# State products of a two-layer kernel: B and C spread by DMA instead of TensorE, the B product on GpSimd instead of VectorE, and four heads per maximum and exponential

## The reference, cut to what matters

```python
def step(h, inp):
    dt_t, B_t, C_t, x_t = inp
    dA = jnp.exp(dt_t[..., None] * A)
    h = dA * h + dt_t[..., None] * B_t[:, None, :] * x_t[..., None]
    y = jnp.sum(h * C_t[:, None, :], axis=-1)
    return (h, y)
```

## Time and profile before

| | before |
|---|---|
| median of 3 runs | 1556.84 us (1555.11 to 1557.42) |
| the profiled execution | 1551.08 us |
| its span | 1549.3 us |
| mean granted TensorE clock | 0.894 |
| DMA, mean over the span | 40 GB/s |

### The profile page before, as it was taken

The page is one execution under the profiler, slowest core; times in us unless marked ns, Lnnn a source line. Parts: engine busy times, 40 slices in busy tenths (PEclk is TensorE's granted clock), DMA queues, the critical chain, the costliest instruction groups (busy, mean ns, idle before and its releaser), DMA issues.

```text
span 1549.3 us, 28028 instructions
## 1 busy us (share of the span) xinstructions
PE 1230.7 (79%) x10568; PEld 841.1 (54%) x10568; DVE 1056.9 (68%) x1741; ACT 734.8 (47%) x1420; POOL 273.4 (18%) x277
## 2 busy tenths in 40 slices
PE   4777877689986998789986998689976997679228
PEld 3554444356753576356753576356844675347118
DVE  2343355977688676867688677977698667966864
ACT  1233444555563645455554645555554644453322
POOL 1000010222012110221012110221013110321250
PEclk9799998889997999789987999899988999799659
DMA  5330010011200211011210211012111121002002
GB/s 199 58 41 1 12 43 28 1 26 39 72 32 14 46 49 60 1 25 39 73 32 15 46 54 54 1 25 56 56 32 23 41 69 32 14 9 82 30 0 72
DMA packets 109587, 62.28 MB, mean 40 GB/s; under 512 B 71248, under 2 KB 91504, under 8 KB 109456
## 3 DMA queue, kind: packets, MB, share of 16 engines
q1 hardware_dynamic: 108448, 56.95, 14.2%
q10 hardware_dynamic: 1008, 3.54, 0.6%
HBM read 53.36 MB, written 6.59 MB: 39 GB/s over the span
## 4 chain that ended last, share of the span: by engine, by line
PE 57%; DVE 21%; issue 9%; ACT 9%; DMA 1%; POOL 1%; SPq 0%; ACTq 0%; DVEq 0%; POOLq 0%
PE strips L813 8%; PE strips L798 7%; PE ps L992 7%; PE ps L980 6%; PE attn_out L826 6%; DVE hb L1461 6%; ACT probs L1085 5%; DVE hb L1456 3%; DVE rowmax_B L1314 3%; PE ps L745 3%; PE attn_out L833 2%; DVE rowmax_A L1314 2%; PE ps L754 2%; DVE work L1428 2%; PE ps L763 2%
## 5 line engine op out<-in xcount | busy, mean ns | idle before, releaser
L1085 ACT ACTIVATE probs<-strips 128x1024 f32<-128x1024 f32 x256 | 251.6, 1021 | 133.1 <-PE strips L813 132.7
L1314 DVE TENSOR_REDUCE rowmax_B<-strips 128x4 f32<-128x1024 f32 x192 | 226.0, 1219 | 77.9 <-PE strips L798 77.7
L813 PE MATMUL strips<-qs_b,ks_b 32*128 32x256 f32 x1536 | 130.0, 459 | 33.0 <-ACT probs L1085 30.5
L798 PE MATMUL strips<-ks_b,qs_b 32*128 32x256 f32 x1536 | 124.7, 443 | 37.4 <-ACT probs L1085 25.2
L1461 DVE TENSOR_TENSOR_SCAN hb<-da,hb 128x1024 f32<-128x1024 f32 x64 | 152.3, 2379 | 2.2
L1547 DVE SCALAR_TENSOR_TENSOR work<-hb,ps 128x512 f32<-128x512 f32 x128 | 87.7, 686 | 88.8 <-ACT hb L1215 88.5
L992 PE MATMUL ps<-ze,w_e 128*128 128x256 f32 x512 | 129.6, 388 | 3.3 <-DVE work L1547 1.9
L980 PE MATMUL ps<-w_e,work 128*128 128x128 f32 x1024 | 125.2, 276 | 0.2 <-DVE work L1547 0.2
L980 PEld LDWEIGHTS ps<-w_e,work 128*128 128x128 f32 x1024 | 122.2, 192 | 5.2 <-issue 2.8
L1215 ACT ACTIVATE hb<-ps 128x512 f32<-128x512 f32 x128 | 75.9, 599 | 103.4 <-PE ps L992 101.4
L1174 ACT ACTIVATE da<-gate,a_neg 128x255 f32<-128x255 f32 x256 | 108.3, 499 | 34.1 <-DVE hb L1461 29.0
(11 more groups left out here) (238 smaller groups left out, 1956.6 us busy)
## 6 DMA issues: line engine op xcount, KB each, us to landing
w_e<-in_w_e SPq DMA_DIRECT2D x128, 256.0 KB, 3.1
qs_a<-a_scr SPq DMA_DIRECT2D x8, 512.0 KB, 4.6
ks_a<-a_scr SPq DMA_DIRECT2D x8, 512.0 KB, 4.9
pos<-t_scr SPq DMA_DIRECT2D x8, 264.0 KB, 10.8
a_scr<-qkv_a SPq DMA_DIRECT2D x16, 128.0 KB, 3.7
qs_b<-maxrow_B SPq DMA_DIRECT2D x96, 4.0 KB
x_in<-in_x SPq DMA_DIRECT2D x8, 128.0 KB, 3.1
a_scr<-ks_a SPq DMA_DIRECT2D x2, 512.0 KB, 6.3
```

The costliest lines, as they stand in the source:

```text
L798: mm = pe.matmul(o, strip(qs, b, kind, g, j, qc * P, P), strip(ks, b, kind, g, j, 0, L), start=True, stop=True)
L813: mm = pe.matmul(o, strip(ks, b, kind, g, j, kc * P, P), strip(qs, b, kind, g, j, 0, L), start=True, stop=True)
L1085: act.activation(probs[:, group % 2, 2 * i:2 * i + 2, :, :].rearrange("p h a b -> p (h a b)"), strips[i][:, :], ACT.Exp).then_inc(s_exp, 1)
L1314: dve.tensor_reduce(out=rowmax[kind][:, b % sides_n, k % 2, 2 * i:2 * i + 2, :], in_=strips[i][:, :].rearrange("p (h q t) -> p h q t", h=2 ...
```

## The change: what it does

- B and C are no longer spread by TensorE. ScalarE copies the 32 rows from PSUM to `bc_rows`, a DMA writes them to DRAM (`bc_scr`), and eight DMAs for each sequence read two rows of B and two of C back with a partition step of zero, 512 KB each, into a ring of four (`bc_all`). All are issued by SP. The bf16 split, `sel` and the matmuls of L933 are gone.
- The B product moves from VectorE to GpSimd (stage `input`), two pairs ahead. The C product stays on VectorE and reads C from SBUF.
- Softplus, the tanh of the experts and `h_t` get tiles of their own, and `ze` gets a second half, so waits of layer one on the experts of the sequence before are gone or later.
- `strips` is one tile of 2048 columns; one `top` and one `exp` do four heads.
- The table of numbers is new, with a lane of its own for what comes after `h_t`.

```diff
+BC_RING = 4
-        CELL += [("max", "B", _g), ("top", "B", _g, 0), ("top", "B", _g, 1), ("rows", "B", _g)]
+        CELL += [("max", "B", _g), ("top", "B", _g), ("rows", "B", _g)]
...
-LAYER1 += [("inproj",), ("conv",), ("xc",), ("bcdt",), ("bc",), ("sp_u",), ("sp_z",)]
-LAYER1 += [("state", _k) for _k in range(NS // 2)]
+LAYER1 += [("inproj",), ("conv",), ("xc",), ("bcdt",), ("bc_write",), ("sp_u",)] + [("bc", _k) for _k in range(BC_RING)] + [("sp_z",)]
+LAYER1 += [("input", 0), ("input", 1)]
+for _k in range(NS // 2):
+    LAYER1 += [("state", _k)] + ([("input", _k + 2)] if _k + 2 < NS // 2 else []) + ([("bc", _k + BC_RING)] if _k + BC_RING < NS // 2 else [])
...
 START = {
-    "one": [0, 24262, 48541, 72825, 97082, 121354, 145602, 169496],
+    "one": [0, 24336, 48715, 73062, 97418, 121814, 146122, 171281],
+    "two": [99, 24430, 48842, 73166, 97539, 121895, 146278, 402809],
...
-        strips = [ctx.enter_context(nc.psum_tensor(f"strips{i}", [P, 2 * 512], F32)) for i in range(2)]
+        strips = ctx.enter_context(nc.psum_tensor("strips", [P, 4 * 512], F32))
...
-        sp_abs = work[:, 0, 0:2, :]
-        sp_max = work[:, 0, 2:4, :]
-        sp_u = work[:, 1, 0:2, :]
-        sp_p = work[:, 1, 2:4, :]
+        bc_rows = sb("bc_rows", [2 * NS, L])
+        bc_all = sb("bc_all", [P, BC_RING, 2, 2, L])
+        sp_abs, sp_max, sp_u, sp_p = (sb(n, [P, CH, L]) for n in ("sp_abs", "sp_max", "sp_u", "sp_p"))
...
-        eh_t = hb[:, :, :, :, :].rearrange("p a c j t -> p a (c j) t")[:, :, 0:2, :]
+        eh_t = sb("eh_t", [P, 2, 2, L])
+        bc_scr = nc.dram_tensor("bc_scr", [2 * NS, L], F32).ap()
...
+            def bc_write(b):
+                sp.wait_ge(*bc_done.at(b))
+                past(sp, hc_done, b - 1, NS // 2 - 1)
+                sp.dma_start(bc_scr, bc_rows[:, :]).then_inc(bc_written.of(b), 16)
+
+            def bc_read(b, k):
+                if k == 0:
+                    sp.wait_ge(*bc_written.at(b))
+                if k >= BC_RING:
+                    sp.wait_ge(*hc_done.at(b, k - BC_RING))
+                i = (b * (NS // 2) + k) % BC_RING
+                src = bass.AP(tensor=bc_scr.tensor, offset=2 * k * L, ap=[[0, P], [NS * L, 2], [1, 2 * L]])
+                sp.dma_start(bc_all[:, i, :, :, :].rearrange("p w j t -> p w (j t)"), src).then_inc(bc_in[i], 16)
...
-            def state(b, k):
-                pe.wait_ge(*bc_steps.at(b, 4))
-                for which, base in (("b", 0), ("c", NS)):
-                    o = take(b, (which, k))
-                    for j in range(2):
-                        mm = pe.matmul(...)
-                    mm.then_inc(s_ps, 1)
...
             def bcdt(b):
+                ready(act, b, "bc")
+                past(act, bc_written, b - 1)
+                act.activation(bc_rows[:, :], bank(b, "bc")[0:2 * NS, 0:L], ACT.Copy).then_inc(bc_done.of(b), 1)
                 ready(act, b, "dt")
-                past(act, acc_done, b - 1, EX)
+                past(act, sp_steps, b - 1, 8)
...
             def state(b, k):
-                ready(dve, b, ("b", k))
-                o = bank(b, ("b", k))[:, :].rearrange("p (o j t) -> p o j t", o=1, j=2).to_broadcast([P, CH, 2, L])
-                dve.tensor_tensor(hk, o, dtx[:, :, :].unsqueeze(2).to_broadcast([P, CH, 2, L]), ALU.mult).then_inc(hb_done.of(b), 1)
                 dve.wait_ge(*hb_done.at(b, k))
                 dve.wait_ge(*da_done.at(b, k))
                 dve.tensor_tensor_scan(flat_h, flat_a, flat_h, 0.0, ALU.mult, ALU.add).then_inc(scan_done.of(b), 1)
                 dve.wait_ge(*scan_done.at(b, k))
-                ready(dve, b, ("c", k))
-                dve.tensor_tensor(hk, hk, o, ALU.mult).then_inc(hc_done.of(b), 1)
+                dve.wait_ge(bc_in[n % BC_RING], 16 * (n // BC_RING + 1))
+                c = bc_all[:, n % BC_RING, 1, :, :].unsqueeze(1).to_broadcast([P, CH, 2, L])
+                dve.tensor_tensor(hk, hk, c, ALU.mult).then_inc(hc_done.of(b), 1)
...
+            def state_input(b, k):
+                pool.wait_ge(*dtx_done.at(b))
+                if k >= 2:
+                    pool.wait_ge(*pair_done.at(b, k - 2))
+                n = b * (NS // 2) + k
+                pool.wait_ge(bc_in[n % BC_RING], 16 * (n // BC_RING + 1))
+                c = bc_all[:, n % BC_RING, 0, :, :].unsqueeze(1).to_broadcast([P, CH, 2, L])
+                pool.tensor_tensor(hb[:, k % 2, :, :, :], c, dtx[:, :, :].unsqueeze(2).to_broadcast([P, CH, 2, L]), ALU.mult).then_inc(hb_done.of(b), 1)
```

More of the change, by code:

```diff
@@ L164 @@
+        "two": [],
     },
@@ L422, in hybrid_layers @@
         xc_done = sig("xc_done", 1)
-        bc_steps = sig("bc_steps", 5)
+        bc_done = sig("bc_done", 1)
+        bc_written = sig("bc_written", 1, 16)
+        bc_in = [one(f"bc_in{i}") for i in range(BC_RING)]
         sp_steps = sig("sp_steps", 9)
@@ L777, in take_strips @@
                     user, was, kind, g = STRIP_LIST[at - 1]
-                    for i in range(2):
-                        if was == "max":
-                            pe.wait_ge(*top_done[kind].at(user, 2 * g + i))
-                        else:
-                            pe.wait_ge(s_exp, EXP_AT[user, kind, g, i] + 1)
+                    if was == "max":
+                        pe.wait_ge(*top_done[kind].at(user, g))
+                    else:
+                        pe.wait_ge(s_exp, EXP_AT[user, kind, g] + 1)
             def strip(tiles, b, kind, g, j, first, n):
@@ L1189, in ffn @@
                 ready(act, b, ("f1", k))
+                if b and k == 0:
+                    ready(act, b - 1, ("y", EX - 1))
                 o = bank(b, ("f1", k))
@@ L1313, in tops @@
                     ready(dve, b - sides_n, ("rows", kind, chunks - 2 + k))
-                dve.tensor_reduce(out=rowmax[kind][:, b % sides_n, k % 2, 2 * i:2 * i + 2, :], in_=strips[i][:, :].rearrange("p (h q t) -> p h q t", h=2, q=2),
+                dve.tensor_reduce(out=rowmax[kind][:, b % sides_n, k % 2, :, :], in_=strips[:, :].rearrange("p (h q t) -> p h q t", h=4, q=2),
                                   axis=AX, op=ALU.max).then_inc(top_done[kind].of(b), 1)
```

200 lines of the change are left out of this document (90 added, 110 removed), and 8 rows, old and new, of the table PLACES.

## The result

The changed kernel takes **1592.46 us** (median of four runs, 1590.05 to 1597.15) where the kernel before takes 1555.97 (1551.09 to 1557.42) beside it: ratio 1.0258, 95% interval 1.0228 to 1.0287. It is 2.6% slower. (The two medians alone give 1.0235, which lies in the interval too; the ratios in this document are those of the recorded comparison of all runs.) The forecast was 1611, slower by 3.5%.

A forecast was written before the change was run, and what follows sets the result against it. VectorE bounds the state phases, TensorE the stretches between. Mixed phases +30 and last phase +27 make +57 on 1551.1, 1608; half the 5.7 to the median gives 1611 us, +3.5%, range 1575 to 1635, 8 in 10 for 1535 to 1655.

The forecast's parts named there:

- GpSimd's B product, 2.35 us: B product of 1024 columns on GpSimd takes 2.35 us, from the slope of its two-operand sums; bounds 1.22 and 2.54.
- The C product excludes GpSimd: C product on VectorE, now with two SBUF operands, excludes GpSimd like the scan; its own length stays 1.22 us.
- rival 1: C product runs beside GpSimd without exclusion: 9.8 us fall out of each phase, 1533 us in all; 13 in 100.
- The last phase, +27: Eighth phase, nothing beside it: instructions and 39 hand-overs add to 69.1 us until y, against 42.15.
- The phase in the mixed part, +9.0 - 3.0 - 1.0 - 0.7: Each of seven mixed phases: exclusion chain 66.5 against 57.5 us, less outside work, queue and four heads: +4.3, together +30.
- What was taken in from outside, and TensorE's queue: Mixed phases: one maximum and one `post_a` taken in, -3.0 us; work formerly queued behind TensorE's spreading matmuls, -1.0.
- Four heads, -0.7 for each phase: Exponentials and maxima over 2048 columns at once are shorter than two of 1024: -0.7 us for each mixed phase.
- Cover of the reads: B and C transfers: 512 KB reads of 4.6 us land before they are needed, so they cost nothing.
- Rival 2: Between phases, uncoupled experts fill TensorE's 9.0 us idle, seven times 63 us: 1548 us; 12 in 100 for faster.
- Rival 3: Large reads delay the maxima's small DMAs, 4.6 us in eight phases: +37, 1648 us; or TensorE's clock falls; 17 in 100.

The follow-up runs named there:

- b_on_vector: The changed kernel with the B product moved back to VectorE, still reading B from SBUF: 1571.93 us, ratio 1.0116.
- both edits: The kernel before, in its own order, with four heads at once and layer one's own tiles, B and C still spread by TensorE: 1546.69 us, ratio 0.998.

## Why the prediction was right, and where its terms were off

**Direction and size.** Slower with 71 in 100, 1611 us against 1592.46, inside the range. The mechanism, exclusion of the two engines, was the right one. That the number came within 19 us is in part luck, since errors in the mixed phases and outside them went against each other, as shown below.

**GpSimd's B product, 2.35 us.** Right: 2.35 at 833.71, and 2.34 as the shortest of 64. The estimate of 2.25, half of the 4497 ns that the Trainium skill (GPSIMD Engine Reference, Performance versus the Vector engine) gives for 2048 columns, was 0.1 short. The figure itself agrees with the rows: 727 and 1267 ns for 256 and 512 columns lie on a line with 187 ns at no columns and 4507 at 2048. Halving took away half of that fixed part.

**The C product excludes GpSimd.** Right, and rival 1 is refuted: 1.23 alone, 2.11 behind a running sum, mean 1.906. b_on_vector shows the same of a B product read from SBUF. By the rule of the Trainium skill (SBUF — State Buffer, Who interferes with whom) it is two SBUF operands that count; the trace agrees, with 2.18 for the pair sum there and 1.27 beside B in PSUM.

**The last phase, +27.** Measured +20.6, so a quarter too much was put on it. My chain added the lengths of instructions that ran alone and 0.05 for each hand-over. For a pair that is 2.35 + 2.28 + 1.23 + 1.26 + 1.26 = 8.38, with hand-overs 8.6. The measured 7.70 is shorter than even the bare sum. The rows show how, counting from end to end: the scan ends 2.14 after the pair sum in place of 2.28 (1498.29 to 1500.43), the running sum 1.06 after the scan in place of 1.26, the C product 1.08 after that in place of 1.23, the B product 2.20 after the C product in place of 2.35. So at each turn 0.14 to 0.20 us of the length do not count, and the hand-overs vanish. An instruction that stands still has already been issued, and my reading is that the first part of it runs while it waits; the rows would look the same if the last part of the one ahead did not exclude any more. The clue stood in the prediction: the running sum of 1.27 "ended 1.07 after the scan". I used that row for the mechanism and not for the size. 0.9 us for each of seven pairs is 6.3, which is the difference.

**The phase in the mixed part, +9.0 - 3.0 - 1.0 - 0.7.** Predicted 66.5 for the chain, measured 64.0 in the mean, so +6.5 in place of +9.0, seven times 2.5 = 17 us. Two errors are in it, and they go against each other. The lengths were added up too high as above: in the last phase, where the chain is closed, dt to the eighth C product took 60.1, so 6.4 less than 66.5. And the chain is not "without holes": the mixed phases are 3.9 longer than those 60.1, of which 3.0 are the stretch behind 836.06 in which neither engine ran an instruction of the chain. Stepping through the order did not find it.

**What was taken in from outside, and TensorE's queue.** I had 4.7 for each sequence; the stretches between phases fell by 2.8 to 4.5 us (113.06 to 110.22 behind the fourth phase). This holds for six of the seven; the last, shorter one fell by 1.3. The reason was only in part the one I gave. The fourth phase now holds 386 matmuls where it held 379 with 32 of spreading among them, so 39 have moved in, and the stretch behind it holds 888 in place of 929. TensorE is busy 3.7 us less there.

**Four heads, -0.7 for each phase.** The lengths were right: 1.875 us for an exponential of 2048 columns (read off: 1.87), and 2.29 for a maximum (2.36 less 0.1). What that gives the kernel is not confirmed. In the order of before the mean of the seven phases fell from 57.5 to 56.7, but the stretches between them grew by as much, and the whole kernel came out 0.2% lower with both edits, with an interval that reaches 1.0001.

**Cover of the reads.** Right: GpSimd was idle 1.7 us in all before its 64 B products, VectorE 2.2 before its C products, and a read of 512 KB landed in 5.3 us in the median, where I had taken 4.6.

**Rival 2**, the uncoupled experts fill TensorE's idle time: refuted. TensorE's idle time between phases is 9.8 us (110.22 - 100.42), and was 9.0.

**Rival 3**, the transfers hold the attention up: not in the changed kernel. TensorE waited 4.7 us in all for `qs_a`, though SyncE stood 124.3 us at reads ahead of such transfers. But the danger was real: misplaced reads cost 1.1% in one of my kernels and 2.4% in the other. Its second half, a lower clock, was not seen in the changed kernel either. The granted clock in the phases is 0.76 to 0.84 after and was 0.74 to 0.83.

**A slip in the sums.** The prediction counts rival 1 at 1611 - 78 = 1533 and later names it 1536; the 3 us move nothing but the lower end of the wide range. The other sums come out as they stand, within rounding.

**How the errors add up.** The terms in the phases were 17 and 6 us too high, and those outside (seven times 4.7, 33 us) took away 8 more than the 24.8 measured. That leaves 16 us too much on the span, 57 against 41.5; the other 3 are the step from the profiled execution towards the median.

## What to carry to other kernels

GpSimd is no second VectorE for work on SBUF: before moving an operation to it, ask of each VectorE instruction beside it whether it reads two operands in SBUF, and add the lengths of both engines as if they were one. Here that sum was 9% too high for a closed chain. A VectorE product with one operand in PSUM ran beside GpSimd at full speed here, so taking matmuls off TensorE, where it waits anyway, can make VectorE slower. In a queue of transfers a read that waits for something can be worse than a large one: put it behind the small transfers that are needed before it is let go.
